# VectorE compares the edges of the group two ahead before it copies q and finds positions

## The reference

```
row, col = src, dst
h    = silu(concat[x[row], x[col], edge_attr] @ eW1 + eb1)      # (50000, 128)
m    = silu(h @ eW2 + eb2)                                      # (50000, 128)
agg  = segment_sum(m, row, num_segments=50000)
u    = silu(concat[x, agg] @ nW1 + nb1) @ nW2 + nb2
out  = layernorm(x + (x + u))
```

## Time and profile before

| | |
|---|---|
| median of 3 runs | 1565.13 us (1563.51 to 1565.40) |
| profiled execution | 1560.06 us, span of its instructions 1558.5 us |
| mean granted TensorE clock | 0.889 |
| PE busy | 1214.8 us (78%) |
| POOL busy | 1046.3 us (67%) |
| DVE busy | 753.9 us (48%) |
| ACT busy | 464.9 us (30%) |

### The profile page before, as it was taken

One profiled execution on the slowest core, in us unless ns is written; L12 is line 12 of the kernel. 1 busy time (PEld: TensorE's weight loads), 2 busy tenths in 40 slices (PEclk: granted clock), 3 DMA queues, 4 the chain that ended last, 5 costly groups with the idle time before them and its releaser, 6 DMA issues.

```text
span 1558.5 us, 21182 instructions
## 1 busy us (share of the span) xinstructions
PE 1214.8 (78%) x6237; PEld 822.9 (53%) x6237; DVE 753.9 (48%) x2820; ACT 464.9 (30%) x846; POOL 1046.3 (67%) x1268
## 2 busy tenths in 40 slices
PE   3813677888898888979888877777777979999895
PEld 3812344454454444645554444444444579888884
DVE  8941244443344343433433433333333458888885
ACT  0000111222232222222222222222222247777774
POOL 8877565665666556656555666666666548899986
PEclk9996698898899888989888887988888979999998
DMA  9997334455565555655655554555454169999994
GB/s 339 413 411 257 94 106 117 140 166 164 158 200 174 160 165 162 191 171 163 185 164 167 158 154 150 164 164 155 155 153 135 53 228 411 410 410 410 407 407 168
DMA packets 183322, 333.48 MB, mean 214 GB/s; under 512 B 25648, under 2 KB 89696, under 8 KB 183205
## 3 DMA queue, kind: packets, MB, share of 16 engines
q1 hardware_dynamic: 136580, 211.68, 40.7%
q0 software_dynamic: 25024, 52.10, 11.3%
q10 hardware_dynamic: 21600, 68.32, 11.1%
HBM read 215.94 MB, written 116.06 MB: 213 GB/s over the span
## 4 chain that ended last, share of the span: by engine, by line
PE 45%; another core or an unknown queue 26%; DMA 8%; issue 7%; ACTq 7%; DVE 3%; ACT 2%; POOL 2%; POOLq 0%; SPq 0%; DVEq 0%
DMA ring<-table 8%; ACTq L782 7%; PE psum L677 6%; PE psum L751 6%; PE psum L721 6%; PE psum L719 5%; PE psum L700 5%; PE psum L733 5%; PE psum L723 5%; PE psum L708 3%; PE psum L766 3%; POOL table L556 1%; PE psum L664 1%; DVE work L1066 1%
## 5 line engine op out<-in xcount | busy, mean ns | idle before, releaser
L556 POOL DMA_INDIRECT table<-qs,pos x391 | 383.1, 980 | 334.8 <-DVE qs L1046 226.5
L508 POOL DMA_INDIRECT ring<-x_d,idx_src x391 | 408.2, 1044 | 119.1 <-issue 119.1
L1001 DVE COPY work<-psum 128x512 f32<-128x512 f32 x98 | 67.8, 692 | 554.4 <-remote 292.2
L677 PEld LDWEIGHTS psum<-work,windows 128*128 128x128 f32 x980 | 176.4, 200 | 147.5 <-issue 130.3
L677 PE MATMUL psum<-work,windows 128*128 128x256 f32 (+1 forms) x980 | 197.2, 350 | 59.0 <-issue 40.0
L700 PE MATMUL psum<-xT_in,w_self 128*128 128x320 f32 x314 | 129.5, 497 | 136.0 <-ACT u_out L803 101.0
L751 PE MATMUL psum<-work,ring 128*128 128x80 f32 x1250 | 157.3, 280 | 28.1 <-DVE work L1066 24.0
L751 PEld LDWEIGHTS psum<-work,ring 128*128 128x128 f32 x1250 | 148.9, 195 | 37.9 <-issue 21.1
L809 ACT ACTIVATE work<-psum,b_e 128x512 f32<-128x512 f32 x98 | 67.4, 687 | 322.0 <-PE psum L723 164.8
L721 PE MATMUL psum<-work,w_src 128*128 128x512 f32 x196 | 133.1, 766 | 36.7 <-DVE work L1001 20.8
L733 PE MATMUL psum<-work,w_e 128*128 128x512 f32 x196 | 122.1, 710 | 21.2 <-ACT work L809 21.2
(11 more groups left out here) (123 smaller groups left out, 1624.4 us busy)
## 6 DMA issues: line engine op xcount, KB each, us to landing
ring<-table SPq DMA_DIRECT2D x79, 528.0 KB, 11.1
table<-empty ACTq DMA_DIRECT2D x9, 4224.0 KB
edge_rows<-edges_dram SPq DMA_DIRECT2D x98, 384.0 KB
windows<-x_wide_d SPq DMA_DIRECT2D x98, 320.0 KB
xT_in<-xT_d SPq DMA_DIRECT2D x78, 320.0 KB
out<-windows ACTq DMA_DIRECT2D x78, 320.0 KB, 6.2
u_dram<-u_out SPq DMA_DIRECT2D x64, 320.0 KB
own_x<-x_d SPq DMA_DIRECT2D x48, 320.0 KB, 8.2
```

The costliest lines, as they stand in the source:

```text
L508: pool.indirect_dma_start(rows, None, x[:, :], bass.IndirectOffsetOnAxis(ap=idx[:, g * TILES + t:g * TILES + t + 1], axis=0)).then_inc(don ...
L556: pool.indirect_dma_start(table[:, :], bass.IndirectOffsetOnAxis(ap=pos[:, g * TILES + t:g * TILES + t + 1], axis=0), q[g % Q][:, t, :], None,
L677: last = nc.tensor.matmul(p_dst[:, tiles], window[g % WINDOWS][:, j, :], pick[g % 2][:, places], start=j == 1, stop=j == 4, skip_group_che ...
```

## The change

In the edge loop DVE's four steps of a group come in another order: `compare_edges(g + 2)` moves from the last place to the second. All instructions, buffers and semaphores stay as they are, and PE, ACT, POOL and SP run the same programs.

```diff
             find_pos(0)
             for g in range(GROUPS):
                 copy_xs(g + 1)
+                compare_edges(g + 2)
                 if g > 0:
                     copy_q(g - 1)
                 find_pos(g + 1)
-                compare_edges(g + 2)
             copy_q(GROUPS - 1)
```

## The result

| | before | after |
|---|---|---|
| median of 4 runs | 1564.32 us (1555.28 to 1565.40) | 1623.57 us (1612.53 to 1627.55) |
| profiled execution, span | 1560.06, 1558.5 | 1612.53, 1611.0 |
| mean granted clock | 0.889 | 0.879 |

The change makes the kernel slower: ratio 1.0381, interval 1.0317 to 1.0445. That is +59 us between the medians and +52.5 between the profiled executions, where +30 was forecast. What follows accounts for the 52.5; the profiled execution after was the fastest of its four.

What follows compares the result with a forecast made beforehand. PE, busy 78% of the span, was taken as the bound, with stops and half clock. Middle +30, late groups +8, start -8 gave +30 on 1560.06, 1590; 5.1 more for the median: 1595 us, own range 1575 to 1625.

Steps and rivals of the forecast that it cites:

- Steps 1 and 2: On DVE, the moved comparisons take 2.6 us, and their own waits, as for edge rows, hold nothing.
- Step 3: On PE, the idle gaps before turn_dst (L677) go: a gain of 32.1 us at most, 0 at least.
- Step 4: On PE, copy_q and find_pos end 2.6 us later where q is not late, but nothing waits: cost 0.
- Step 5: POOL begins a group's scatters 2.6 us later, no cost as a wait; its lost pause then brings PE's stop one group sooner.
- The first two rivals: Edge loop: gaps go and stretches keep four groups, 1533 or 1549, chance 0.28; or gaps return in stops, 1565, chance 0.14.
- a lock: On PE in the edge loop, a gap that goes comes back in the stop: 1565 us, chance 0.14.
- The third: In the edge loop POOL becomes the bound, at 11.6 and late 13.2 us a group: 1609 us, chance 0.10.
- The middle: Groups 14 to 71 of the edge loop: stretches of three groups instead of four, +17 to +46 us, taken as +30.
- The start: When the loop begins, turn_dst(2) no longer waits 8.16 us for pick: 0 to -8 us, taken as -8.
- The late groups: Groups 72 to 92, seven stretches of three: the flush after POOL's run moves by some 2.0 us or nothing; 0 to +14, taken +8.
- The number of stops: In the middle groups, stretches of three instead of four groups make 4.8 more stops of PE.
- A stop: PE stands still before a self matmul (L700) for 5.7 us, and the half clock costs 5.1 us more.

Runs made afterwards that it cites:

- e9: The changed kernel, without a further edit, on another chip (13): 1624.67 us against 1560.3 for the kernel before, ratio 1.0416.
- e12: Kernel before, DVE's order kept, POOL's scatters of group g also waiting for the comparisons of group g+3; chip 15: 1657.83 us against 1559.22, ratio 1.0648.
- e1: Kernel before, DVE's order kept, POOL's scatters of group g also waiting for the comparisons of group g+3; chip 5: 1350.17 us, ratio 1.0000.

## Why the prediction was right, and where its size was off

The mechanism forecast was: the gaps go, POOL starts later, its runs lose their pauses, stops come one group sooner. Each link is in the trace. The median of 1623.57 lies inside the range of 1575 to 1625, but only 1.4 us from its end, and the change cost twice what was forecast; that the range held is partly luck.

**Steps 1 and 2, right.** From the first comparison to copy_q it is 845.12 - 842.51 = 2.61 us; 2.6 was taken. (The comparisons are eight DVE instructions, two L1011, L1015, four L1018 and L1023, and not seven; the sum goes by the time and is not touched.) DVE still waits for edge rows twice, 18.8 us in all, when the loop begins.

**Step 3, right, and at its upper bound.** The idle time before L677 went from 32.1 to 0.0. As a gain it is not seen, since PE's idle time short of the pauses stayed at about 20 us in groups 14 to 72.

**Step 4, right but for a side effect.** Nothing waits for copy_q or find_pos on PE. But L708 has 16.8 us of idle time between groups 14 and 97, where it had 1.0, 14.6 of it behind ACT's L815: mT too comes late when PE's completions do.

**Step 5, right in its chain.** First scatter 4.2 us after copy_xs at 841.90 (4.5 forecast). The transposes of 849.43, which end when that run is 4 us old, are copied on time at 850.07, as forecast; the pause of 0.9 us that was to follow in the run is not there at all. POOL's runs of indirect DMAs between 185 and 1240 us, counted from the trace with a pause under 0.75 us as part of the run, are 56 with a mean of 14.3 us, where they were 75 of 11.1; in e9 58 of 13.9, in e12 53 of 14.6. The stretches have three groups. That POOL's later start is what costs was an inference when it was forecast. e12 shows that this start alone, with DVE's order left as it was, lengthens the runs and costs 98.6 us; that it is all of the change's cost is not shown.

**The first two rivals, wrong.** Stretches did not keep four groups. Nor was it a lock, in which a gap that goes comes back in the stop and the time stays at 1565. The third, POOL as the bound (1609), is nearest by its number, but not by its mechanism: POOL is idle for 381.0 us ahead of its scatters.

**What was mis-sized: the sum of +30.**

- *The middle*, +30 forecast with bounds +17 and +46: +45.7 in the profiled execution, +27.7 in e9's. Once the stretches repeat, at groups 32 to 68, the rate is what was forecast: 413.3 us against 394.5, +0.5 a group, and 34.1 a stretch is the lower of the two lengths. The miss lies in groups 14 to 32, 218.5 against 193.5 us, +1.4 a group, beyond the bound of 0.8. There the kernel before did a little better than in the groups behind (10.75 us a group against 10.96), and the changed one did clearly worse (12.1 against 11.5), at a clock of 0.85 against 0.89. I carried the rate of the middle over to these groups. Why the changed kernel is slower there is open; e9's has 210.0 us, +0.9 a group.
- *The start*, -8 forecast: +1.9. turn_dst(2) at 156.04 waits for nothing where it waited 8.16 us, but copy_xs of that group comes at 177.09 and came at 176.71. The wait was taken off a path that another wait ended.
- *The late groups*, +8 forecast with bounds 0 and +14: +0.2 there, and +4.7 behind the loop, where nothing was forecast.
- *The number of stops* was right: 4.8 more were forecast for the middle, and there are 5 more pauses. Their price was not. The idle time in pauses rose by 7.0 us for each of the five, and half clock cost 2.1 us more in all, where 5.7 and 5.1 for each stop were put down; and 13 us were taken off for gaps, whose place other gaps took.
- *A stop*, priced at 5.7 us standing and 5.1 for the clock, 10.8. The 5.1 was too high already: PE was busy for 8.49 of the 10.2 us at 0.50, so the clock cost 4.2 and a stop 9.9. After, it is 7.6 standing (867.16) and 3.24 us of PE work at half speed, so 1.6, which is 9.2. A longer stop comes with a shorter slow stretch, of which more falls into the idle time. 3 x 8.17 + 9.2 = 33.7 of the 34.1.

The Trainium skill, TensorE: Matmul & The Clock Gate, HAM oscillation, counts half of the throttled time as lost. The trace disagrees: before, 4.2 of 10.2 us, and after, 1.6 of 6.8, since only the part in which PE works costs anything.

The last piece of the +59 lies between executions: the profiled ones are +52.5 and +41.9 (e9), and the medians, whose executions left no trace, +59 and +64. Why most executions are slower than the two profiled is open.

## What to carry to other kernels

An engine that is off the critical path can still set the pace through when it works: before moving a copy later, look at what the engine that it releases does to the others, and not only at who waits for it. A gap that a reordering closes is worth its length only if the larger, rarer stop behind it stays where it is; count stops per stretch, before and after. And test a mechanism by that mechanism alone (delay POOL, leave DVE's order), on the chip on which the effect was seen.

## What the runs showed of the hardware

**PE's completions come late while POOL issues indirect DMAs, on some chips only.** For each matmul from 185 to 1240 us that raises a semaphore I took the time from its modelled end to the semaphore's next event in the trace, if there is one within 12 us, at full granted clock, by the age of POOL's run at that end. The share that is over 0.5 us late:

```
age of POOL's run     before (1560)   after (1611)   e12 (1656)   e1 (chip 5, 1351)
POOL idle             0.16            0.26           0.35         0.00
under 3.0 us          0.12            0.23           0.36         -
3.0 to 4.5 us         0.35            0.29           0.30         -
4.5 to 6.0 us         0.80            0.80           0.67         -
6.0 to 7.5 us         0.98            0.94           0.61         -
7.5 to 10.5 us        0.80            0.94           0.95         -
over 10.5 us          1.00            1.00           1.00         0.01 (638 events)
```

The median lateness over 10.5 us is 6.6, 7.8 and 7.8 us in the first three. The age sorts the completions, but not cleanly, and in e12 less so. A part of the shares at low age is an artefact: on these chips the trace lacks semaphore events (DVE raises its semaphores 1409 times; before has 1133 events of that, e1 lacks none), and an event of the next matmul then stands in for the one that is missing. That is also why copy_xs has idle time under "issue". What the events cannot hide is the start of the copy, 8.0 us behind its transposes at 866.20. On chip 5 POOL's run never ends in the loop, and 1 in 100 is late. e1 in time order, where POOL has been issuing for hundreds of us:

```profile
599.23 0.98 POOL L508 DMA_INDIRECT ring<-x_d,idx_src  x1 [0.30 <-issue]
...
600.94 0.60 PE L665 MATMUL psum<-ident,ring 128*128 128x128 f32 x4
...
601.58 0.69 DVE L1002 COPY work<-psum 128x512 f32<-128x512 f32 x1 [1.54 <-PE psum L665]
601.80 0.98 POOL L508 DMA_INDIRECT ring<-x_d,idx_src  x1 [0.30 <-issue]
```

The transposes end at 601.54 and are copied at 601.58. So a long run of POOL's is not enough by itself; something that differs between these chips must be added. The two levels of this kernel are 209 us apart (1560 against 1351), far more than the change; how much of that is lateness, and what differs between the chips, no run shows. Whether the lateness needs POOL's gathers, its scatters or both was not tried on a chip that has it.
